# Last attention of a two-layer block on one core: TensorE's transposes three score tiles behind, its value products four

## The reference, cut to what matters

```python
q = jnp.einsum('btc,hdc->bhtd', x, Wq)
k = jnp.einsum('btc,hdc->bhtd', x, Wk)
...
v = jnp.einsum('bthe,bted->bhtd', mix_v, proj_v)
scores = jnp.einsum('bhid,bhjd->bhij', q * scale, k)
probs = jax.nn.softmax(scores, axis=-1)
attn = jnp.einsum('bhij,bhjd->bihd', probs, v)
...
res = jnp.einsum('bthe,bthd,efd->bthf', mask_o, attn, Wo)
return res.sum(axis=2)
```

## Time and profile before

| what | value |
|---|---|
| time, median of 3 runs | 3498.43 us (3491.45 to 3499.49) |
| time of the profiled execution | 3494.1 us |
| span of the profiled execution | 3492.3 us |
| TensorE busy, page | 2708.3 us (78%) |
| VectorE, ScalarE, GpSimd busy, page | 1943.5, 1459.6, 1033.4 us |
| mean granted TensorE clock | 0.883 of full |
| S, L1547, all four batches | 277.7 us busy, 2.8 idle before |
| T, L1525 | 157.2 us busy, 145.9 idle before, released by L1063 |
| V, L1538 | 258.1 us busy, 0.0 idle before |

### The profile page before, as it was taken

How to read it: one execution, slowest core, us unless ns; L and a number is a source line. 1 busy time by engine, 2 the same in 40 slices (tenths; PEclk the granted TensorE clock), 3 DMA queues, 4 the chain that set the end, 5 groups by cost and what they waited for, 6 DMA issues and landing times.

```text
span 3492.3 us, 37809 instructions
## 1 busy us (share of the span) xinstructions
PE 2708.3 (78%) x13116; PEld 1579.1 (45%) x13116; DVE 1943.5 (56%) x4693; ACT 1459.6 (42%) x2326; POOL 1033.4 (30%) x418
## 2 busy tenths in 40 slices
PE   0575869879693996879598879689789689788689
PEld 0432223333232563356276346367346367346367
DVE  8454121211112111684877684887684887685877
ACT  3042746556471222451254461255451245461245
POOL 1022000000001113360760460670460680360680
PEclk9987989889796998789799789899879899889889
DMA  2046542424023111002000102000102000002000
GB/s 87 15 167 174 88 56 39 64 38 65 2 74 103 50 46 34 26 6 89 19 1 7 31 3 91 19 1 7 31 1 94 19 1 7 25 1 88 0 1 7
DMA packets 88479, 146.57 MB, mean 42 GB/s; under 512 B 16724, under 2 KB 58840, under 8 KB 88248
## 3 DMA queue, kind: packets, MB, share of 16 engines
q1 hardware_dynamic: 80760, 134.57, 14.8%
q0 software_dynamic: 7504, 9.35, 1.4%
HBM read 121.17 MB, written 22.88 MB: 41 GB/s over the span
## 4 chain that ended last, share of the span: by engine, by line
PE 58%; DVE 23%; ACT 6%; issue 6%; DMA 2%; POOLq 1%; SPq 1%; POOL 1%; DVEq 0%; ACTq 0%
PE ps L1547 6%; PE ps L1389 6%; PE ps L1538 6%; PE ps L1152 4%; PE ps L1163 4%; PE ps L1525 3%; PE ps L1419 3%; DVE sb_arena L664 3%; ACT sb_arena L877 2%; DVE sb_arena L666 2%; DVE sb_arena L2066 2%; PE ps L1325 2%; PE ps L1172 2%; PE ps L1487 2%; PE ps L1338 2%
## 5 line engine op out<-in xcount | busy, mean ns | idle before, releaser
L877 ACT ACTIVATE sb_arena<-ps 128x1024 f32<-128x1024 f32 x416 | 403.2, 1021 | 239.7 <-PE ps L1152 237.6
L2066 DVE MAX8 sb_arena<-sb_arena 128x8 f32<-128x60 f32 (+1 forms) x1728 | 247.2, 205 | 164.3 <-ACT sb_arena L976 164.1
L1389 PE MATMUL ps<-sb_arena 128*128 128x512 f32 (+1 forms) x512 | 288.7, 650 | 25.0 <-ACT sb_arena L976 13.0
L1802 DVE COPY sb_arena<-ps 128x512 f32<-128x512 f32 x64 | 44.3, 692 | 457.4 <-PE ps L1163 457.4
L1547 PE MATMUL ps<-sb_arena 128*128 128x512 f32 x512 | 277.7, 627 | 2.8 <-ACT sb_arena L1050 2.8
L1063 ACT ACTIVATE sb_arena<-ps,sb_arena 128x512 f32<-128x512 f32 x256 | 175.4, 685 | 237.8 <-DVE sb_arena L2215 237.8
L1525 PE MATMUL ps<-sb_ident,sb_arena 128*128 128x128 f32 x1024 | 157.2, 277 | 145.9 <-ACT sb_arena L1063 145.9
L777 POOL TENSOR_TENSOR sb_arena<-sb_arena 128x1601 f32<-128x1601 f32 x56 | 173.8, 3104 | 305.6 <-DVE sb_arena L2054 305.6
L1152 PE MATMUL ps<-sb_arena 96*128 96x512 bf16 x832 | 236.1, 392 | 31.2 <-issue 24.8
L664 POOL TENSOR_TENSOR sb_arena<-sb_arena 128x1024 f32<-128x1024 f32 x96 | 232.0, 2417 | 88.3 <-DVE sb_arena L2170 77.2
L1538 PE MATMUL ps<-sb_arena 128*128 128x64 f32 x2048 | 258.1, 270 | 0.0
(11 more groups left out here) (336 smaller groups left out, 5151.7 us busy)
## 6 DMA issues: line engine op xcount, KB each, us to landing
sb_arena<-in_ctxT SPq DMA_DIRECT2D x13, 1601.0 KB, 7.2
sb_arena<-k_spill SPq DMA_DIRECT2D x96, 208.0 KB, 8.3
sb_arena<-in_dft SPq DMA_DIRECT2D x5, 2048.0 KB, 7.9
k_spill<-sb_arena SPq DMA_DIRECT2D x12, 832.0 KB, 5.2
sb_arena<-in_w SPq DMA_DIRECT2D x16, 512.0 KB, 4.7
sb_arena<-in_idft SPq DMA_DIRECT2D x4, 2048.0 KB, 9.9
sb_arena<-in_wf SPq DMA_DIRECT2D x8, 1024.0 KB, 13.1
sb_arena<-q_spill SPq DMA_DIRECT2D x96, 64.0 KB, 9.9
```

The source lines that it names most:

```text
L877: A(probs0[:, 2 * (m % 4):2 * (m % 4) + 2, :], ps[:, 2 * (m % 2):2 * (m % 2) + 2, :], ACT.Exp).then_inc(pair_probs, 1)
L1389: mm(ps[:, j, 0:w], q1z[:, h, t * P:(t + 1) * P], kT1[:, c0:c0 + w], start=True, stop=False)
L2066: ins = V.max(cand[:, n % 2, 8 * j:8 * j + 8], s_sb[n % 4][:, c0:c0 + w])
```

## The change

TensorE's turns run from 0 to 67, and turn n does S(n), T(n-3), V(n-4). ScalarE's turn n does C(n-3) and then E(n). VectorE's order, the buffers and all waits of the single steps stay as they are.

```diff
@@ ACT @@
-                for n in range(NG + 2):
-                    if n >= 2:
-                        m = n - 2
+                for n in range(NG + 3):
+                    if n >= 3:
+                        m = n - 3
                         act.wait_ge(p2T_done, nth(b, p2T_done, m + 1))
                         if m >= 2:
                             act.wait_ge(o2_done, nth(b, o2_done, m - 1))
@@ PE @@
-                for n in range(NG + 3):
+                for n in range(NG + 4):
                     if n < NG:
...
-                    if 2 <= n < NG + 2:
-                        turn_p2(n - 2)
-                    if n >= 3:
-                        value2(n - 3)
+                    if 3 <= n < NG + 3:
+                        turn_p2(n - 3)
+                    if n >= 4:
+                        value2(n - 4)
```

## The result

The changed kernel takes 3508.56 us (median of 10 runs, 3507.3 to 3510.96), the kernel before 3496.01 us in the 10 runs beside it. The ratio is 1.0035, with a 95% interval of 1.0025 to 1.0045: 12.5 us slower, where 8.8 us faster was forecast. The time lies above the stated range of 3481 to 3500. The profiled execution took 3507.3 us.

A forecast was written before the change was run, and what follows sets the result against it. A stage was taken as a stall set by VectorE, a steady part by TensorE and an end by VectorE. Stall 0, start 0, steady 0 and end -8.8 gave 3489.6 us against the median (3485.3 against the profiled run); range 3481 to 3500.

The forecast's parts named there:

- The stall covers S(3): Stage start: S(3) runs inside T(0)'s wait of about 36 us and costs 0; uncovered it would cost 1.91 us.
- C(0) behind E(2) is hidden: ScalarE at the stage's start: C(0) ends by about 1753.2 us, before V(0) needs it at 1753.70; delay zero.
- Nothing in the steady part: Steady slots: they stay 2.19 us, and the 0.79 us stall stays because V still meets a late VectorE; 0 us.
- The end moves by a whole slot: Stage end: VectorE's block from M(63) on comes 2.19 us earlier, 8.8 us over four stages.
- The gap shrinks to 2.5 us: TensorE's idling between the last V and the transposes of z falls from 3.80 to about 2.5 us.
- Rival A: Stage end: the shorter gap keeps the clock at full, saving another 1.4 us a stage; 3484.0 us, chance 0.20.
- So the whole chain, and everything after it up to the meeting of the engines, moves by 2.19 us.: Stage end: VectorE's chain from M(63) on and what follows come 2.19 us earlier, with TensorE's inputs in time.
- up to 0.8 us a stage either way: Output products after the end's gap: the clock's drop may come earlier or later, 3.2 us in all.
- rival P: Posed with the follow-up runs: the new tile order itself harms what follows, and dead work costs only its own time.
- Rival C: VectorE against GpSimd in each stage: four more heads lose 0.79 us each, 1.0 us worse a stage; 3502.4 us, chance 0.06.
- T(0) stays at 1750.23: First stage's start: VectorE's mixing sets the stall's length and doesn't move, so T(0) keeps its time.

The follow-up runs named there:

- after_again: The changed kernel run again with no edit: 3510.77 us, ratio 1.0036 to the kernel before.
- pad: The changed kernel plus 2.15 us of dead VectorE work at the end of each of the first three last attentions: 3501.63 us, ratio 1.0014.
- after_pad2: The changed kernel plus 1.2 us of dead VectorE work after each of the first three last attentions: 3493.95 us, ratio 1.0003.
- warm_end: The changed kernel plus unread TensorE products only between the last V and the transposes of z: 3495.41 us, ratio 1.0011.
- before_again: The kernel before run again with no edit: 3498.5 us, ratio 1.0008.

## Why the prediction was wrong

By its own steps:

- **The stall covers S(3).** Right. T's wait is 35.3 instead of 36.2 us as its longest, as S(3) fills part of it. C(0) and V(0) follow T(0) as they did, and the stage's start is otherwise the same to 0.02 us.
- **C(0) behind E(2) is hidden.** Right: V(0) is still 3.47 us behind T(0).
- **Nothing in the steady part, "and the 0.79 us stay".** Nearly right in the sum, wrong in the working. Slots are 2.19 us. The stall of 0.79 us is gone from its place, and in the first stage 0.29 and 0.25 us are lost at other tiles (none in after_again). In the fourth stage, which lost nothing before, 0.59 us are lost behind an L2184 that took 2.21 us; no L2184 of that stage had taken more than 0.51. V has 0.3 us of idling for C in all, where it had none.
- **The end moves by a whole slot, 2.19 us a stage, 8.8 in all.** Right in mechanism, and the size came within a tenth: 2.08, 2.33, 2.09 and 1.61 us, 8.1 in all. The fourth is short by the 0.59 us just named. In after_again it is 4.24, 2.23, 2.09 and 1.54, 10.1 in all: T(2) of the first stage comes 1.6 us earlier there, at a granted clock of 0.79 instead of 0.53 (1756.7 to 1763.2 us in both traces), an uncertainty that I had named and left at nothing in the sum.
- **The gap shrinks to 2.5 us.** Right (2.52). Rival A's condition, that the clock stays up there, didn't come: behind the shorter gap it fell too (0.50 from 1899.58 to 1901.00), and in the changed kernel's last stage the output products take longer (14.42 us from z to the end instead of 13.64).
- **"So the whole chain, and everything after it up to the meeting of the engines, moves by 2.19 us."** This was taken to hold behind the meeting too, and there it failed. I priced the clock in the stage alone, "up to 0.8 us a stage either way", by the eight output products of rows 8. The cross attention behind the stage was not looked at. It opens with waits of 2.22, 2.52 and 1.60 us on a TensorE that is busy for 75 to 84% of the time, and its scores run at either level. Behind the changed stage, stretches of 382.7 and 384.6 us became 391.5 and 390.3. That is +14.0 and +19.5 us in the two traces, against the -8.1 and -10.1 of the stages. The term that I bounded by 3.2 us, the clock, thus measured four to six times as much, and in a place that the sum didn't hold. The repeats, the openings and the filled waits show that the loss is the clock's. How the change brings it about stays open. No run separates the earlier end of the stage from the shorter gap ahead of z. Pair by pair, new order against old with the same additions, the three stretches together are longer by 14.0 and 19.5 us without any, by 6.8 and 6.7 with dead work (pad, after_pad2), by 8.2 with three waits filled, and by 1.6 in one pair and -1.7 in the other with all four filled. So rival P's sign held in every pair but that with all waits filled.
- **Rival C** had the right sign and the wrong place: the meetings of VectorE with GpSimd moved to other tiles, but the slots' losses come to 1.1 us over all stages in one trace and 0.6 in the other, where they were 0.8.

Open are some 2 to 6 us of the 12.5, what the 6.7 and 10.2 us behind the first T(0) leave. Also wrong was "T(0) stays at 1750.23": both traces of the changed kernel reach it at 1756.7, those of before at 1750.2 and 1753.5, though TensorE's work ahead of it is the same but for S(3), which the stall covers. Three other kernels with the change in all four stages and the same code up to there (pad, after_pad2, warm_end) reach it at 1753.90, 1747.45 and 1752.85, so the new order doesn't fix it. Between before_again and after_again, on one chip, TensorE's first product is 0.4 us later, the first product of L1487 in this batch (near 1635 us) 0.9, its last 2.6, and T(0) 3.2. About half of it thus arises in these 32 products, at a granted clock of 1.00 in one (1636 to 1641 us) and 0.76 in the other (1637.5 to 1642.5). Whether that is chance or the program's own was not tried further.

## What to carry to other kernels

A saving is not passed on unchanged when what follows keeps TensorE busy only in part: such a stretch runs at either clock level, and here a stage that was 2.3 us shorter was followed by a stretch that was 8.8 us longer. So when a kernel is to be compared by tenths of a per cent, look in the trace at the granted clock of the stages behind the change as well as at the stage itself, and price them by their rows at both levels. Cut the traces at fixed instructions: in the kernel before the pieces repeat within 0.02 us where whole executions scatter by 10 (3491.45 to 3502.99). And where waits of 2 us stand in such a stretch, it pays to fill them (here nine unread products at three places gave 0.9% to the kernel before). That alone didn't show what the reordering is worth: with nine the two orders measured alike, and only with four more products in the wait that the change itself had shortened did it show its 10 us.

## What the runs showed of the hardware that I had not expected

- The clock's pattern repeats from run to run: seven stretches of some 143 and 385 us in two traces of the kernel before, on different occasions, agree within 0.02 us, though they hold dozens of changes of the clock. In the changed kernel five of the seven agree within 0.1 us, and the first stretch came out at 385.86 and at 391.28.
- Added work can make a kernel faster: three unread products a batch brought the changed kernel from 1.0035 to 0.9976 of the kernel before, with 15 to 19 us less from the first T(0) to the end. With 3.6 us of dead VectorE work it measured 1.0003, but only 0.7 to 4.2 us of that lie behind the first T(0).
- The best kernel of the study, warm_after5, is the changed one with thirteen unread products a batch: 0.9868 (0.9853 to 0.9884) of the kernel before. Its mean granted clock is 0.894 to 0.896 of full, against 0.883 before and 0.876 in the profiled execution of the changed kernel.
